# One set of statistics for two norms, and triangle solves by columns, in a two-layer transformer kernel

## The reference, cut to what matters

```python
x = x + _L0_ffn_ref(...)                 # the two best experts of each of two groups
z = _layernorm(x)                        # (x - m) / sqrt(v + 1e-5), kept as the residual of the block
# inside the block:
h = (z - mean(z)) * rsqrt(var(z) + 1e-5) * g + b
q, k, v = h @ Wq * Dh**-0.5, h @ Wk, h @ Wv      # heads of 16
k = k / (norm(k) + 1e-6)
beta, gate = sigmoid(h @ Wb), sigmoid(h @ Wg)
# step by step over the sequence, per head:
S = S * gate_t
S = S + beta_t * outer(k_t, v_t - k_t @ S)
o_t = q_t @ S
```

## Time and profile before

| | us |
|---|---|
| median of 3 runs (4370.62 to 4377.01) | 4375.18 |
| the profiled execution | 4372.27 |
| its span, first to last instruction | 4370.5 |

### The profile page before, as it was taken

How to read it: one execution, slowest core, us unless ns; L and a number is a source line. 1 busy time by engine, 2 the same in 40 slices (tenths; PEclk the granted TensorE clock), 3 DMA queues, 4 the chain that set the end, 5 groups by cost and what they waited for, 6 DMA issues and landing times. The chain is left out here.

```text
span 4370.5 us, 116097 instructions
## 1 busy us (share of the span) xinstructions
PE 3585.2 (82%) x41174; PEld 1864.3 (43%) x41175; DVE 2564.7 (59%) x5363; ACT 2101.4 (48%) x4016; POOL 1193.8 (27%) x2453
## 2 busy tenths in 40 slices
PE   8699999999999999606869675606697898699999
PEld 5222322233223222404646434405676565344578
DVE  7788888888888888641212384592354443334333
ACT  2488888888888888403334232204300222343322
POOL 1222222222222221243358444204432232111000
PEclk9799999999999999858989876557755999799999
DMA  1000000000000004434665333436423000310253
GB/s 52 7 6 6 6 6 6 5 6 6 6 6 6 5 6 185 140 124 134 203 193 160 104 121 105 152 98 211 145 75 89 29 0 13 137 74 0 64 179 132
DMA packets 280102, 328.52 MB, mean 75 GB/s; under 512 B 36128, under 2 KB 201248, under 8 KB 279968
## 3 DMA queue, kind: packets, MB, share of 16 engines
q1 hardware_dynamic: 246160, 280.75, 20.2%
q0 software_dynamic: 13328, 37.77, 2.6%
q10 hardware_dynamic: 20480, 8.40, 0.7%
HBM read 181.59 MB, written 135.79 MB: 73 GB/s over the span
## 5 line engine op out<-in xcount | busy, mean ns | idle before, releaser
L942 DVE TENSOR_REDUCE att_maxes<-att_ps_m 128x1 f32<-128x512 f32 x2048 | 1308.5, 686 | 231.1 <-PE att_ps_m L786 228.3
L897 ACT ACTIVATE att_prob<-att_ps_s 128x512 f32<-128x512 f32 x2048 | 1105.4, 600 | 223.4 <-PE att_ps_s L796 210.5
L796 PE MATMUL att_ps_s<-att_q_t,att_k_t 99*128 99x512 bf16 x2048 | 687.3, 386 | 8.7 <-ACT att_prob L897 7.9
L807 PE MATMUL att_ps_o<-att_prob,att_v_h 128*32 128x512 f32 x4096 | 546.4, 605 | 0.7 <-ACT att_prob L897 0.7
L784 PE MATMUL att_ps_m<-att_k_t,att_q_t 48*128 48x512 bf16 x1024 | 399.3, 390 | 16.2 <-DVE att_maxes L942 11.5
L786 PE MATMUL att_ps_m<-z_sb 48*128 48x512 bf16 x1024 | 399.5, 390 | 0.0
L784 PEld LDWEIGHTS att_ps_m<-att_k_t,att_q_t 48*128 48x128 bf16 x1024 | 94.6, 92 | 610.3 <-DVE att_maxes L942 508.2
L695 POOL CAST att_max_parts<-att_neg_max 128x4 bf16<-128x4 f32 x128 | 24.7, 193 | 1155.3 <-DVE att_neg_max L949 1155.3
L1567 DVE TENSOR_TENSOR experts_h<-experts_gs,experts_ps_g 128x128 f32<-128x128 f32 x192 | 55.3, 288 | 443.5 <-ACT experts_gs L1548 441.7
L796 PEld LDWEIGHTS att_ps_s<-att_q_t,att_k_t 99*128 99x128 bf16 x2048 | 157.8, 96 | 281.2 <-ACT att_prob L897 134.5
L1520 PE MATMUL experts_ps_g<-w_gu,experts_x_t 128*128 x768 | 222.1, 413 | 31.3 <-issue 15.1
(11 more groups left out here) (362 smaller groups left out, 6741.4 us busy)
## 6 DMA issues: line engine op xcount, KB each, us to landing
slots_x<-zeros SPq DMA_DIRECT2D x97, 256.0 KB, 3.2
experts_xs<-slots_x SPq DMA_DIRECT2D x48, 512.0 KB
slots_y<-experts_y SPq DMA_DIRECT2D x48, 512.0 KB
logits_t<-sstat_logit SPq DMA_DIRECT2D x64, 256.0 KB
xf_t<-logits_t SPq DMA_DIRECT2D x8, 2048.0 KB
proj<-comb_pr SPq DMA_DIRECT2D x8, 1600.0 KB
mix_pr<-proj SPq DMA_DIRECT2D x32, 400.0 KB
gram_qk_in<-proj SPq DMA_DIRECT2D x32, 256.0 KB
```

Source lines behind the costliest of these rows:

```text
L796: pe.matmul(ps_s[bank(p, i)][:, :], k_t[0:ROWS, p, tile * P:(tile + 1) * P], q_t[0:ROWS, p, chunk * W:(chunk + 1) * W], start=True, stop=T ...
L807: mm = pe.matmul(ps_o[i * VW:(i + 1) * VW, :], v_h[:, p, group * GK + i, :], prob[:, (j * GK + i) % (RING * GK), :], start=(group == 0), s ...
L897: nc.scalar.activation(prob[:, i % (RING * GK), :], ps_s[bank(p, i)][:, :], ACT.Exp, scale=SCALE).then_inc(expd.sem, 1)
L942: v.tensor_reduce(maxes[:, p, tile, c:c + 1], ps_m[bank(p, i)][:, :], X, ALU.max).then_inc(reduced.sem, 1)
```

## The change

In the gathering phase the statistics of z are no longer taken. Both standard deviations come from the variance v of x2: `veps` gets two entries, v + 1e-5 and v (1 + 1e-5) + 1e-10, and one power of 8 elements on a partition gives the factors of z and hn. Both are then formed from x2 in the middle of the pass, hn first, behind the bias of tiles 0 and 1 of the group before. GpSimd's fetches run two groups ahead and are no longer split. In the lanes phase the triangle is solved by columns: first every column's own entries are set (15 negations), then for j = 1 to 14 one multiplication and one subtraction on j x 8 x (15 - j) elements.

```diff
-            def root(t, of, which, steps):
-                pool.wait_ge(of.sem, of.at(t, 2 * GT + 1))
-                pool.tensor_tensor(rstd[:, which, :], veps[:, which, :], neg_half[:, :], ALU.pow).then_inc(steps.sem, 1)
-
-            fetch(0, 0, GT * NY)
+            def root(t):
+                pool.wait_ge(norm_z.sem, norm_z.at(t, 2 * GT + 2))
+                pool.tensor_tensor(rstd[:, :, :], veps[:, :, :], neg_half[:, :, :], ALU.pow).then_inc(roots.sem, 1)
+
+            fetch(0)
+            fetch(1)
             for t in range(N):
-                more = t + 1 < N
-                if more:
-                    fetch(t + 1, 0, 4)
-                root(t, norm_z, 0, root_z)
-                if more:
-                    fetch(t + 1, 4, 7)
-                root(t, norm_h, 1, root_h)
-                if more:
-                    fetch(t + 1, 7, GT * NY)
+                root(t)
+                if t + 2 < N:
+                    fetch(t + 2)
...
-                v.tensor_scalar(veps[:, which, :], mv[:, which, :, 1], EPS, None, ALU.add).then_inc(steps.sem, 1)
+                v.tensor_scalar(veps[:, 0, :], mv[:, :, 1], EPS, None, ALU.add).then_inc(norm_z.sem, 1)
+                v.tensor_scalar(veps[:, 1, :], mv[:, :, 1], 1.0 + EPS, EPS * EPS, ALU.mult, ALU.add).then_inc(norm_z.sem, 1)
...
                 if t < N:
-                    centre(t, norm_z, root_z, x2[:, p], z[:, p], 0)
-                    v.wait_ge(norm_z.sem, norm_z.at(t))
-                    moments(t, norm_h, z[:, p], 1)
+                    v.wait_ge(roots.sem, roots.at(t))
+                    v.wait_ge(turned.sem, turned.before(t))
+                    centre(t, p, norm_h, hn, 1)
+                    centre(t, p, norm_z, z, 0)
                 if 1 <= t <= N:
                     add_bias(late, pl, (2, 3))
                 if t >= 2:
                     scale_keys(t - 2, p)
-                if t < N:
-                    v.wait_ge(turned.sem, turned.before(t))
-                    centre(t, norm_h, root_h, z[:, p], hn[:, p], 1)
...
-                for t in range(1, CL):
-                    v.wait_ge(t_ts.sem, t_ts.at(r, 2 * (t - 1)))
-                    terms = prod[:, 0:t * HR * t].rearrange("q (i h j) -> q i h j", i=t, h=HR)
-                    v.tensor_tensor(terms, t_t[:, p, 0:t, :, 0:t], gains[:, r, t, :, 0:t].unsqueeze(1).to_broadcast([P, t, HR, t]),
+                for j in range(CL - 1):
+                    below = gains[:, r, j + 1:CL, :, j].rearrange("q t h -> q h t")
+                    v.tensor_scalar(t_t[:, p, j, :, j + 1:CL], below, -1.0, None, ALU.mult).then_inc(t_ts.sem, 1)
+                for j in range(1, CL - 1):
+                    done = CL - 1 + 2 * (j - 1)
+                    below = gains[:, r, j + 1:CL, :, j].rearrange("q t h -> q h t").unsqueeze(1).to_broadcast([P, j, HR, CL - 1 - j])
+                    terms = prod[:, 0:j * HR * (CL - 1 - j)].rearrange("q (i h t) -> q i h t", i=j, h=HR)
+                    v.wait_ge(t_ts.sem, t_ts.at(r, done))
+                    v.tensor_tensor(terms, t_t[:, p, 0:j, :, j:j + 1].to_broadcast([P, j, HR, CL - 1 - j]), below,
                                     ALU.mult).then_inc(t_ts.sem, 1)
-                    v.wait_ge(t_ts.sem, t_ts.at(r, 2 * t - 1))
-                    v.tensor_reduce(t_t[:, p, 0:t, :, t], terms, X, ALU.add, negate=True).then_inc(t_ts.sem, 1)
+                    v.wait_ge(t_ts.sem, t_ts.at(r, done + 1))
+                    v.tensor_tensor(t_t[:, p, 0:j, :, j + 1:CL], t_t[:, p, 0:j, :, j + 1:CL], terms,
+                                    ALU.subtract).then_inc(t_ts.sem, 1)
```

More of the change, by code:

```diff
@@ L1599, in phase_combine @@
         hn = ph.sb("hn", [P, 2, GT, D])
-        stats = ph.sb("stats", [P, 2, GT, 6])
-        mv = ph.sb("mv", [P, 2, GT, 2])
+        stats = ph.sb("stats", [P, GT, 6])
+        mv = ph.sb("mv", [P, GT, 2])
         veps = ph.sb("veps", [P, 2, GT])
         rstd = ph.sb("rstd", [P, 2, GT])
-        neg_half = ph.sb("neg_half", [P, GT])
+        neg_half = ph.sb("neg_half", [P, 2, GT])
         h_t = ph.sb("h_t", [P, KD, GP])
@@ L1623, in phase_combine @@
         added = ph.steps("added", GT * NY)
[L1624 to L1627, removed]
+        norm_z = ph.steps("norm_z", LN + 1)
+        norm_h = ph.steps("norm_h", GT)
+        roots = ph.steps("roots")
         kept = ph.steps("kept", 2)
@@ L1662, in _, with fetch @@
         def _(pool):
-            for s in (root_z, root_h):
-                s.prime(pool)
-            pool.memset(neg_half[:, :], -0.5).then_inc(set_up, 1)
+            roots.prime(pool)
+            pool.memset(neg_half[:, :, :], -0.5).then_inc(set_up, 1)
             pool.wait_ge(set_up, 1)
-            def fetch(t, first, last):
+            def fetch(t):
                 p = t % 2
                 pool.wait_ge(added.sem, added.before(t))
-                for iy in range(first, last):
+                for iy in range(GT * NY):
                     i, y = divmod(iy, NY)
@@ L1721, in combine, with moments, centre @@
                                                before, ALU.mult, ALU.add).then_inc(added.sem, 1)
-            def moments(t, steps, src, which):
+            def moments(t, p):
                 for i in range(GT):
-                    v.bn_stats(stats[:, which, i, :], src[:, i, :]).then_inc(steps.sem, 1)
+                    v.bn_stats(stats[:, i, :], x2[:, p, i, :]).then_inc(norm_z.sem, 1)
                 for i in range(GT):
-                    v.wait_ge(steps.sem, steps.at(t, i + 1))
+                    v.wait_ge(norm_z.sem, norm_z.at(t, i + 1))
                     hold(v, gate)
-                    v.bn_aggr(mv[:, which, i, :], stats[:, which, i, :]).then_inc(steps.sem, 1)
-                v.wait_ge(steps.sem, steps.at(t, 2 * GT))
-                v.tensor_scalar(veps[:, which, :], mv[:, which, :, 1], EPS, None, ALU.add).then_inc(steps.sem, 1)
-            def centre(t, steps, roots, src, dst, which):
-                v.wait_ge(roots.sem, roots.at(t))
+                    v.bn_aggr(mv[:, i, :], stats[:, i, :]).then_inc(norm_z.sem, 1)
+                v.wait_ge(norm_z.sem, norm_z.at(t, 2 * GT))
+                v.tensor_scalar(veps[:, 0, :], mv[:, :, 1], EPS, None, ALU.add).then_inc(norm_z.sem, 1)
+                v.tensor_scalar(veps[:, 1, :], mv[:, :, 1], 1.0 + EPS, EPS * EPS, ALU.mult, ALU.add).then_inc(norm_z.sem, 1)
+            def centre(t, p, steps, dst, which):
                 for i in range(GT):
-                    v.tensor_scalar(dst[:, i, :], src[:, i, :], mv[:, which, i, 0:1], rstd[:, which, i:i + 1],
+                    v.tensor_scalar(dst[:, p, i, :], x2[:, p, i, :], mv[:, i, 0:1], rstd[:, which, i:i + 1],
                                     ALU.subtract, ALU.mult).then_inc(steps.sem, 1)
@@ L1770, in _ @@
                     v.wait_ge(added.sem, added.at(t))
-                    moments(t, norm_z, x2[:, p], 0)
+                    moments(t, p)
                 if t >= 2:
@@ L1837, in keep_h @@
                     nc.scalar.copy(h_t[:, k, :], ps_t[k][:, :]).then_inc(h_ready.sem, 1)
-                act.wait_ge(norm_h.sem, norm_h.at(t))
+                act.wait_ge(norm_z.sem, norm_z.at(t))
                 hold(act, gate)
@@ L2068, in phase_lanes @@
         g_in = ph.sb("g_in", [P, 2, CL, 2, 2, LW // 2])
-        prod = ph.sb("prod", [P, (CL - 1) * HR * (CL - 1)])
+        prod = ph.sb("prod", [P, (CL // 2) * HR * (CL // 2)])
         t_t = ph.sb("t_t", [P, 2, CL, HR, CL])
@@ L2074, in phase_lanes @@
         sums = ph.steps("sums", 2)
-        t_ts = ph.steps("t_ts", 2 * (CL - 1))
+        t_ts = ph.steps("t_ts", CL - 1 + 2 * (CL - 2))
         stored = ph.transfers("stored", 2)
```

## The result

The changed kernel took 4320.87 us (median of 4 runs, 4319.69 to 4325.01) beside 4376.1 for the kernel before (4 runs, 4370.62 to 4380.0): ratio 0.9876, 95% interval 0.9859 to 0.9893. The forecast was 4321.5. The two profiled executions took 4325.01 and 4372.27 us, spans 4323.3 and 4370.5.

What follows compares the result with a forecast made beforehand. Gathering was taken as bound by a loop over PE and DVE, lanes by DVE's instructions alone. Savings of 30.5 and 23.2 us, 53.7 together, gave 4318.6 us for the profiled execution, 4321.5 for the median; range 4300 to 4346.

Steps and rivals of the forecast that it cites:

- The loop: Gathering, groups 1 to 7: early hn cuts the period from 21.6 to 17.3 us, saving 25.8 us over six periods.
- The power: Gathering, GpSimd: one power of 8 elements takes 1.2 us instead of two of 1.05; only group 0 pays it.
- tenths: Gathering start: the first power waits behind 16 gathers and is late by nothing or by tenths of a us.
- Group 0: Gathering, first group: hn comes 4.7 us earlier without z, second statistics and second power ahead of it.
- The gathers: Gathering, GpSimd: fetching two groups ahead costs nothing, at most 1 us at the start; later gathers end before the next power.
- The tail: Gathering from projection 7 on (biases, two rounds of keys, stores): same order as before, no change counted.
- Lanes: Lanes phase: a round's triangle falls from 26.3 to 20.5 us, 5.8 us saved, 23.2 us in four rounds.
- The 0.6 ns of the forecast: Lanes phase on DVE: price per element of reading gains with a step of 128 words, 3.3 us a round.
- early rows bring nothing: Rival for gathering: only DVE's 1.75 us a pass is gained, 14 us there, total time 4338 us; chance 0.06.
- the clock stays low: Rival for gathering: PE stays at 1.2 GHz, period 25.9 us, 4382 us; chance 0.05, shared with steps beyond GpSimd's price.
- stepped reads are dear: Rival for lanes: steps cost 1.5 ns an element, 3.6 us gained in all four rounds, 4341 us; chance 0.19.
- the clock is full throughout: Rival for gathering: PE stays at 2.4 GHz, DVE bounds, 35 us gained there, 4317 us; chance 0.22, shared with free steps.

Runs made afterwards that it cites:

- e3_hn_last: The changed kernel with hn put back behind the keys at the end of the pass: 4405.15 us, 0.9942 of the kernel before.
- e4_copies_first: The changed kernel with ScalarE's copies of the turned rows moved ahead of the squares of the previous group: 4367.14 us, 0.9859 of the kernel before.
- e2_gather_only: The kernel before with only the gathering phase changed: 4405.86 us, 0.9947 of the kernel before.
- e9_after_again: The changed kernel run once more without any edit, on another chip: 4380.56 us, 0.9876 of the kernel before.
- e5_plain_reads: The changed kernel with the lanes multiplications reading unit-stepped rows of t_t instead of stepped gains: 4369.24 us, 0.9853 of the kernel before.
- e11_step16: The changed kernel with the lanes multiplications reading gains at a step of 16 words instead of 128, triangle not solved: 4378.91 us, one run.

## Why the prediction came out right

**The total.** 4321.5 was forecast and 4320.87 measured. So close a hit is luck: the interval of the ratio is some 7.5 us wide on either side, and terms that were off cancelled, as shown below.

**The loop.** Right by its steps. The mid-pass hn took keys and hn out of the loop, ScalarE's order kept the copies behind the squares, and from last bias to projection it was 3.73 us, the number taken from pass 1. The period was 17.6 where 17.3 was forecast. In the steady groups it was 17.2 to 17.5 with projections of 12.4 to 12.7, for 12.56 taken; one group had 13.87, and its period was 18.64. So 24.2 us were saved for 25.8. `e3_hn_last` shows that the place carries it, `e4_copies_first` that ScalarE's order holds the rest.

**The power.** Eight elements took 1.68 us, not 1.2: the row of 4 elements had been read as mostly fixed cost without a second row to show it. It is hidden from group 2 on, as argued. In group 0 it is not: POOL's power, and hn waiting for it, in the changed kernel:

```profile
2490.57 1.68 POOL L1678 TENSOR_TENSOR comb_rstd<-comb_veps,comb_neg_half 128x8 f32<-128x8 f32 x1
...
2496.30 2.86 POOL L1671 DMA_INDIRECT comb_y_in<-slots_y,pos  x1 [0.30 <-issue]
...
2504.20 1.69 POOL L1678 TENSOR_TENSOR comb_rstd<-comb_veps,comb_neg_half 128x8 f32<-128x8 f32 x1
```

```profile
2492.30 1.59 DVE L1729 TENSOR_SCALAR comb_hn<-comb_x,comb_mv,comb_rstd 128x256 f32<-128x256 f32 x4 [2.24 <-POOL comb_rstd L1678]
...
2505.92 1.58 DVE L1729 TENSOR_SCALAR comb_hn<-comb_x,comb_mv,comb_rstd 128x256 f32<-128x256 f32 x4 [1.17 <-POOL comb_rstd L1678]
```

`veps` of group 0 was there at 2490.05, the power started at 2490.57, behind the last gather: the "tenths". Group 0 gained 3.8 us (first bias copy to projection: 16.85 before, 13.1 after), not 4.7: 0.5 from the power and 0.5 from its late start.

**The gathers.** "End well before `root(t + 1)`" was wrong in group 1. There PE's first projection comes early, eight gathers (one of 2.86 us) ended at 2504.2, and `veps` had been there since 2500.4. hn of group 1 waited 1.17 us. It cost a few tenths: the gap before that projection was 0.45 us longer than the later ones.

**The tail.** Costed at nothing, it cost 1.4 us in this execution: the last projection took 14.06 us, for 12.61 before. By windows the clock of that projection was 0.78, and within an earlier one it was 0.72 in the first 6 us and 1.00 after. It is no property of the change: at least one such slow projection stands in every trace of this gathering phase, in group 4 of `e2_gather_only`, in group 5 of `e9_after_again`, and there the last one took what it took before:

```profile
2675.10 12.71 PE L1803 MATMUL comb_ps_p<-comb_w_s,comb_h_t 128*128 128x512 f32 x32 [3.88 <-ACT comb_h_t L1828]
```

Gathering as a whole: 3.8 + 24.2 - 1.4, and 0.8 from faster bias matmuls at the start (4.92 us for 5.70), less 0.1 in the period of group 0: 27.3 by these rounded terms for the 27.1 of the windows.

**Lanes.** Right by its sum, 19.9 us a round for 20.5. The negations took 2.1 for 2.3 + 0.6, where the 0.6 is their part of the 3.3 for stepped reads; the 28 dependent instructions took 17.8 for 14.9 + 2.7 = 17.6. So the negations are the term that was off most, 0.8 us a round. They overlapped more than was taken, and they show no price for the step: their means grow from 170 ns for 8 elements to 283 for 120, 1.0 ns an element, as much as unstepped elements cost. The multiplication at j = 7 took 0.92 us, forecast 0.89, the subtraction 0.63. The Trainium skill ("Vector Engine (DVE) Microarchitecture Reference", section 5.2, Measured stream behaviour) puts one source that hops far at 1.73 ns a column against 1.05, 0.68 more. The trace agrees: 0.71, and 0.66 at the step of 16.

The 0.6 ns of the forecast was right by luck. It came from 172 - 167 ns between a multiplication and a reduction of 8 elements, read as the price of the step. But the two instructions differ by as much where the multiplication reads both sources in runs of 15 adjacent words, in the kernel before at 1800 elements:

```profile
L2128 DVE TENSOR_TENSOR lanes_prod<-lanes_t_t,gains 128x1800 f32<-128x1800 f32 x4 | 8.1, 2034 | 0.1
L2131 DVE TENSOR_REDUCE lanes_t_t<-lanes_prod 128x120 f32<-128x1800 f32 x4 | 8.1, 2029 | 0.1
```

Again 5 ns, so they are a difference between the two instructions and no step price, and the row held no evidence for 0.6. Any price from nothing to GpSimd's 2.1 ns was open by the rows of the kernel before; only the rows of the changed kernel, `e5_plain_reads` and `e11_step16` fix it.

**The rivals.** That early rows bring nothing fell with `e3_hn_last`. That the clock stays low fell with the windows (0.89 over the loop, 0.79 before). That stepped reads are dear fell at 0.71 ns. That the clock is full throughout did not come either; even with the copies first it was 0.93, and there DVE decided at 16.3, where the rival had put the bound at 16.5.

The errors of both halves had opposite signs, 3.4 us too much for gathering and 2.5 too little for lanes, so that the sum came out better than its parts: luck too. The windows of the two phases give 52.8 us, the medians 55.2, the profiled executions 47.2. Open: why the executions differ by some 5 us before gathering, and why single gathers take 2 to 2.9 us in place of 0.95.

## What to carry to other kernels

In a loop over in-order engines, don't ask when an operand is ready but what stands ahead of its consumer in that engine's list: by the traces the moved norm gave some 24 us, and two lines moved in ScalarE's list gave 11 to 14 more. An instruction can be moved early only if the wait that it brings along is covered too, or it holds up what is queued behind it; saved work on an engine that waits gives next to nothing alone and may still be what makes such a move pay. Where a trace shows the new situation once, in a first or last pass, take its number for the loop. And before a small difference between two kinds of instruction is read as the price of one property, look whether it is there without the property too.

## What the runs showed of the hardware

- GpSimd's power over 8 elements a partition takes 1.68 us, over 4 elements 1.05: 0.16 us for each element more between these two sizes.
- A multiplication of two tensors on DVE pays 0.66 ns an element for one source with a step of 16 words on every element, and 0.71 with 128. Writing and reading in runs of one costs about as much: the last subtraction of a round (112 elements, runs of 1) took 0.35 us, the first (runs of 14) 0.28. A multiplication by a constant that reads the same column shows no such price: 170 ns for 8 elements, 283 for 120.
- Negations that don't wait for each other overlap: the means of the 15 add up to 3.3 us, and they took 2.08.
- On ScalarE the sigmoid behind the squares brings a table load of 1.28 us into every group.
- With 4.9 us between projections PE was granted 0.89 of its clock over groups 1 to 7, with 1.8 us (and a wait of some 2 us inside) 0.93, with 8.35 us 0.79; from 0.89 to 0.93 PE's time for 240 matmuls fell by 3.2 us.
